# Two rope products written in place in PSUM, and the banks handed back after the rope sums, in a fused attention and feed-forward kernel

## The reference

```python
qkv = x @ w_qkv.T                              # 16 heads of 32
q = q * cos + _rotate_half(q) * sin            # the rope, the same for k
k = k * cos + _rotate_half(k) * sin
scores = jnp.einsum('bhqd,bhkd->bhqk', q, k) * scale
scores = jnp.where(keep, scores, -jnp.inf)     # 0 <= row - column < 64
out = jnp.einsum('bhqk,bhkd->bhqd', softmax(scores), v)
x = layernorm(x + out @ w_out.T)
gate = silu((x @ w_gate) * s_gate); up = (x @ w_up) * s_up
x = layernorm(x + ((gate * up) @ w_down) * s_down)
```

## Time and profile before

| what | value |
|---|---|
| time, median of 3 executions | 1167.32 us (1166.16 to 1168.19) |
| profiled execution, first to last instruction (its span) | 1164.2 us |
| median of the runs less the span | 3.1 us |
| PE busy | 1154.0 us, 99% |
| DVE busy | 984.6 us, 85% |
| POOL busy, ACT busy | 587.3 us, 584.4 us, 50% each |
| granted TensorE clock | 1.000 of full speed |

### The profile page before, as it was taken

How to read it: one execution, slowest core, us unless ns; L and a number is a source line. 1 busy time by engine, 2 the same in 40 slices (tenths; PEclk the granted TensorE clock), 3 DMA queues, 4 the chain that set the end, 5 groups by cost and what they waited for, 6 DMA issues and landing times.

```text
span 1164.2 us, 25539 instructions
## 1 busy us (share of the span) xinstructions
PE 1154.0 (99%) x8433; PEld 567.9 (49%) x8433; DVE 984.6 (85%) x2821; ACT 584.4 (50%) x1640; POOL 587.3 (50%) x563
## 2 busy tenths in 40 slices
PE   9999999999999999999999999999999999999998
PEld 4344446444464444644455444554445444464444
DVE  7899998898987899879998899897898988986434
ACT  3953883048820588105880169701686027950330
POOL 0775684156731667326771367613676236752330
PEclk9999999999999999999999999999999999999999
DMA  9999786366562765617656096561964537734000
GB/s 295 173 175 252 137 166 160 66 88 137 111 149 55 110 131 107 145 41 128 132 97 141 37 146 119 101 132 46 155 123 88 131 63 137 120 73 109 19 2 36
DMA packets 352077, 134.80 MB, mean 116 GB/s; under 512 B 309840, under 2 KB 332496, under 8 KB 351952
## 3 DMA queue, kind: packets, MB, share of 16 engines
q1 hardware_dynamic: 334976, 106.86, 49.6%
q0 software_dynamic: 10560, 17.30, 5.1%
q10 hardware_dynamic: 6416, 9.00, 2.1%
HBM read 32.19 MB, written 8.39 MB: 35 GB/s over the span
## 4 chain that ended last, share of the span: by engine, by line
PE 97%; DVE 1%; ACT 1%; issue 1%; POOL 0%; POOLq 0%; DVEq 0%
PE bank L842 61%; PE bank L1058 18%; PE bank L848 10%; PE bank L984 3%; PE bank L964 2%; PE bank L864 1%; PE bank L1080 1%; ACT bank L1243 1%; PE bank L873 0%; PE bank L1069 0%; PE bank L948 0%; DVE wd L1373 0%; ACT wu L1186 0%; DVE ffn_tmp L1530 0%; ACT fuse L1186 0%
## 5 line engine op out<-in xcount | busy, mean ns | idle before, releaser
L842 PE MATMUL bank<-x1T,wg 128*128 128x512 f16 (+1 forms) x1032 | 242.5, 378 | 0.0
L842 PE MATMUL bank<-x1T,wu 128*128 128x512 f16 x1024 | 241.9, 379 | 0.0
L1243 ACT ACTIVATE bank<-bank,neg_max,qk_scale 128x128 f32<-128x128 f32 x512 | 220.5, 435 | 7.8 <-DVE neg_max L1558 6.1
L1058 PE MATMUL bank<-wd,fuse 128*128 128x512 f16 (+2 forms) x1056 | 222.7, 373 | 0.0
L660 POOL TENSOR_TENSOR fuse<-ffn_tmp,fuse 128x512 f16<-128x512 f32 x128 | 149.7, 1170 | 117.5 <-ACT fuse L1186 116.8
L742 POOL TENSOR_TENSOR fuse<-fuse 128x512 f16<-128x512 f32 x116 | 137.7, 1218 | 74.9 <-ACT fuse L1186 72.8
L1058 PEld LDWEIGHTS bank<-wd,fuse 128*128 128x128 f16 x1056 | 101.9, 98 | 118.0
L842 PEld LDWEIGHTS bank<-x1T,wu 128*128 128x128 f16 x1024 | 100.1, 98 | 120.7
L655 POOL TENSOR_TENSOR xT_sb<-probs,xT_sb 128x512 f16<-128x512 f32 x112 | 129.6, 1158 | 44.5 <-ACT xT_sb L1186 44.4
L842 PEld LDWEIGHTS bank<-x1T,wg 128*128 128x128 f16 x1032 | 96.3, 98 | 113.9 <-issue 4.0
L1196 ACT ACTIVATE ffn_tmp<-bank,tanh_scale 128x512 f32<-128x512 f32 x128 | 88.2, 689 | 100.0 <-PE bank L842 76.8
(11 more groups left out here) (235 smaller groups left out, 1621.5 us busy)
## 6 DMA issues: line engine op xcount, KB each, us to landing
v_cross<-v_own SPq DMA_DIRECT2D x64, 128.0 KB, 2.4
out<-x ACTq DMA_DIRECT2D x31, 256.0 KB, 2.0
xT_sb<-xT SPq DMA_DIRECT2D x30, 256.0 KB, 4.1
qkT<-x SPq DMA_DIRECT2D x28, 256.0 KB, 3.8
wg<-w_gate POOLq DMA_DIRECT2D x7, 1024.0 KB, 5.2
wu<-w_up POOLq DMA_DIRECT2D x7, 512.0 KB, 6.0
wqkv<-w_qkvT SPq DMA_DIRECT2D x8, 256.0 KB, 6.3
wg<-w_gate POOLq DMA_DIRECT2D x1, 2048.0 KB, 8.4
```

Of the source, the lines that this page charges most:

```text
L842: last = pe.matmul(dst, lhsT, rhs, start=(i == 0), stop=(i == len(pairs) - 1))
L1058: last = pe.matmul(dst[:, cols], fuse[:, s, z, rows], wd[:, s, cols], start=(s == 0 and z == 0), stop=(s == STEPS - 1 and z == 1))
L1243: last = act.activation(unit, unit, ACT.Exp, bias=neg_max[:, s % 2, h // 3, h % 3:h % 3 + 1], scale=qk_scale[:, 2:3], accum_out=row_sum[:, ...
```

## The change

In tiles 1 to 7 (`ffn` true) the order of the four products becomes 3, 0, 1, 2. Products 3 (even * sin) and 1 (odd * sin) still go to SBUF. Products 0 (even * cos) and 2 (odd * cos) come second in their bank, and are written back over the bank that they read. The sums then read one bank and one SBUF place each and write to SBUF as before. So the banks are in use until the sums are done, and the three places on PE that waited for `rope_read` before they reuse a bank wait for `rope_done` now. Tile 0's own rope and its waits stay, and so does the wait of the DMA that loads new tables. The number of instructions stays.

```diff
@@ project_v
-                    wait(rope_read, pe, a, j // 2)
+                    wait(rope_done, pe, a, j // 2)
@@ scores
                 elif ffn:
-                    wait(rope_read, pe, a, 2 if s == 0 else NB - 1)
+                    wait(rope_done, pe, a, 2 if s == 0 else NB - 1)
@@ rope_products
                 for part in parts:
-                    i = (0, 3, 1, 2)[part]
+                    i = ((3, 0, 1, 2) if ffn else (0, 3, 1, 2))[part]
                     src = (even, odd, odd, even)[i]
-                    last = dve.tensor_tensor(free_view(place[i], heads), free_view(src, heads), table(i), ALU.mult)
+                    dst = src if ffn and part % 2 else place[i]
+                    last = dve.tensor_tensor(free_view(dst, heads), free_view(src, heads), table(i), ALU.mult)
@@ rope_sums
                 place = rope_place(j, ffn)
+                even, odd = qk_banks(j, ffn) if ffn else (place[0], place[2])
                 wait(rope_read, dve, a, j)
-                dve.tensor_tensor(place[0], place[0], place[1], ALU.subtract)
-                done(rope_done, dve.tensor_tensor(place[2], place[2], place[3], ALU.add))
+                dve.tensor_tensor(place[0], even, place[1], ALU.subtract)
+                done(rope_done, dve.tensor_tensor(place[2], odd, place[3], ALU.add))
```

## The result

The changed kernel takes 1170.81 us (median of 6 runs, 1169.29 to 1171.69) against 1166.88 us for the kernel before on the same chips (6 runs). The ratio is 1.0029, with a 95% interval of 1.0019 to 1.0040: slower by 2.2 to 4.7 us. The profiled execution has a span of 1169.1 us, 4.9 more than before.

What follows compares the result with a forecast made beforehand. The prediction took PE, busy 99% of the span, as the bound. It summed 2.2 (tile 0's end) + 0.1 (start of round 1) + 0 (rounds) = 2.3 us on 1167.3, giving 1169.6 us; range 1167.9 to 1171.2 us.

Steps and rivals of the forecast that it cites:

- PE bounds the rounds, and DVE's relief does not reach the end: Rounds: PE runs its own list, 141.92 us each; DVE's saving becomes idle time before the scores, no gain or cost.
- The rival with a faster kernel: Rounds: if DVE bounded them, up to 14.5 us would go less the 2.3, giving 1155.1 us; chance 0.05.
- The sums lose their tail: DVE's rope sums, seven tiles: with one bank operand they fall to about 0.69 us each, 14.5 us gone from DVE.
- Prices of bank operands: DVE's products written to banks and sums reading banks: 0 to 0.02 us an instruction, under 1.2 us in all.
- Tile 0's end: the one real wait: project_v of tile 1's block 0 waits for sums behind keep_o and two finish_x1: 2.21 us stall, lasting until the end.
- sums that stay stretched: Rival: scores 1 of round 1 waits 1.6 us, 3.8 in all, 1171.1 us; shares 0.11 with two other cases.
- The forecast's mechanism: Whole kernel: the stall at tile 0's end plus a little at round 1's start, 2.0 to 2.6 us; chance 0.76.
- the wait priced too low, in the case with 0.11: A PE wait costing more than forecast; no size given; chance 0.11 together with stretched sums or dear in-place writes.
- the border of 0.2%: Whole kernel: 0.2%, 2.3 us, about what measurement can tell from no change; within 0.48, slower 0.47, faster 0.05.
- Start of round 1: Scores 1 of round 1, one tile of seven: DVE's chain hangs on PE; 0 to 0.14 us lost, 0.1 taken.
- No stall in tile 0: Rival, tile 0's end: first two finish_x1 run before POOL's subtraction, project_v on time; 0 to 0.2 us, 1167.4; chance 0.08.

Runs made afterwards that it cites:

- experiment 6: Changed kernel, but block 0 of tile 1 keeps the old products and sums over SBUF and its rope_read hand-over: 1167.17 us, ratio 0.9998.
- experiment 7: Changed kernel with tile 1 block 0's rope sums directly behind their products and POOL's weight subtraction behind its first two split_low: 1166.86 us, ratio 0.9996.
- Experiment 2: Kernel before with only the three waits changed to rope_done, all products and sums over SBUF as before: 1171.45 us, ratio 1.0040.
- Experiment 3: Changed kernel with 11 extra matmuls on PE ahead of project_v of tile 1's block 0, result overwritten: 1169.27 us, ratio 1.0019.
- experiment 5: Changed kernel with the rope sums of tile 1's block 0 put between the two finish_x1 in DVE's list: 1168.96 us, ratio 1.0017.
- experiment 8: Changed kernel with 5 extra matmuls on PE ahead of project_v of tile 1's block 0: 1169.95 us, ratio 1.0024.
- experiment 1: Changed kernel with tile 1 block 0's rope sums directly behind their products, ahead of keep_o and the two finish_x1: 1167.34 us, ratio 0.9997.
- experiment 4: Changed kernel with POOL's weight subtraction in tile 0 moved behind its first two split_low of tile 1's block 0: 1167.37 us, ratio 1.0001.

## Why the prediction came out as it did

- **PE bounds the rounds, and DVE's relief does not reach the end.** Right. The rounds are the same 141.92 us, DVE's idle time before the scores' maxima grew from nothing to 1.93 us, and experiments 6 and 7 keep the relief and stay within 0.13% of the kernel before by their intervals. The rival with a faster kernel is out.
- **The sums lose their tail.** Right: 28 sums of each kind at 680 to 689 ns. Experiment 2, where they keep it, has the 1.6 us wait at scores 1 that the prediction priced at 1.6 for this rival. DVE as a whole got 12.0 us and not 14.5: the sums alone did shrink by 14.7, but other operations were stretched in turn, one split_x1 by 0.96 us and finish_x1 by 0.32. The other 1.4 us were not traced to their operations. Nothing of the time hangs on them.
- **Prices of bank operands.** Right: 5 ns for a product, nothing for a sum. The Trainium skill's figures for a PSUM source ("VectorE: DVE Perf Modes", section on the TRN2 errata) gave an estimated 0.065 us more for each sum, and that is not seen: 689 and 680 ns with a bank, 693 and 683 as the medians without.
- **Tile 0's end: the one real wait.** The place, the cause and the first part of the price were right: 2.2 us forecast, 2.42 measured. finish_x1 took 3.59 us in place of 3.27, and the passage from DVE to PE about 0.05 us (sums done at 92.97, project_v at 93.02) in place of the 0.14 that was taken for it; the two errors offset in part.
- **The term that was missing.** The forecast carried the stall to the end as it stood. It left out what the standstill does to PE itself: 1.70 us for the project_v behind it, on the lower clock. Of the ledger's 4.46 us that is 38%. This is the main reason why the kernel came out 3.9 us over the kernel before and not 2.3. Experiments 3, 5 and 8 each take the lower clock away, in two ways, and 1.7 to 1.8 us go with it between project_v and weigh_v 15. The trace before did show a fall, but where it costs nothing: at its end, 4.4 us after the last matmul, the granted clock goes to 0.50. No matmul at the lower clock stood in it from which to price one. The Trainium skill says it in words ("TensorE: Matmul & The Clock Gate", Part 1): the gate passes only part of the pulses by default, and PE's own activity releases it. The trace after agrees with 0.50 behind the gap. It should have been weighed as a rival.
- **The range held partly by luck.** Its upper end, 1171.2, was put there for sums that stay stretched, and they did not. The forecast with the 1 us that was given to the spread of the runs ends at 1170.6, and 1170.81 lies above that. The forecast's mechanism alone was given 2.0 to 2.6 us with a chance of 0.76, and the loss was 3.9; it belongs to the wait priced too low, in the case with 0.11. The forecast also started from 1167.3, and the kernel before has a median of 1166.88 here, which hides 0.4 us of the miss. Against the border of 0.2% that the prediction names, the ratio of 1.0029 is slower, the outcome that it held for slightly the less likely of the two (0.47 to 0.48); the interval's lower end, 1.0019, just touches the border.
- **Start of round 1.** Forecast 0 to 0.14 us, measured 0.34. The step that failed is that DVE's chain hangs on PE there. Before, DVE waited 0.23 us for PE at 109.84. After, it did not wait at all: a `split_x1` on DVE, a pass over two SBUF tensors, took 1.64 us in place of 0.68 beside one of POOL's split_low, and the chain ran 0.28 us later against PE than before. In experiment 1 that operation took 0.68 and scores 1 lost 0.10; in experiments 4 and 7 it took 1.64 and 1.65, and scores 1 lost 0.33 and 0.34. DVE meets POOL there within less than 0.1 us, and which of the two goes first decides about 0.25 us. Where DVE's operation began 0.05 us ahead of POOL's (before, 106.39 and 106.44; experiment 1, 106.96 and 107.01) it took 0.68. Where it began 0.06 or 0.07 us behind (after, 110.63 and 110.56; experiments 2 to 8 alike) it took 1.64 or 1.65.
- **No stall in tile 0**, the rival on the other side: its condition did not come up in the changed kernel, and experiment 4, which makes it true, gives the time that it named, 1167.4 us.

Open: how long PE must stand still before it costs the clock. The ends of the traces speak against a fixed length. There PE stands still after its last matmul, and the clock falls 2.0 us later in experiment 5, 3.0 in 1, 4.4 in the kernel before and 5.3 in the changed kernel. In tile 0 it fell 2.9 us after PE had stopped (changed kernel) and 3.5 us (experiment 2), both times with PE at work again. So a gap of 2.35 us may be spared in another execution, and one of 2 us may not. Two of the changed kernel's six executions have spans of 1167.5 and 1167.6, and the other four 1168.9 to 1169.4. That would fit a fall that does not come each time, but no trace of the short ones shows it.

## What to carry to other kernels

When a buffer's release moves from the last reader's first half to a later instruction on the same engine, read what stands between the two in that engine's list, at every place where they are called: the rounds had 0.9 us of slack or more, and the hand-written end of tile 0 had none. Price a new PE gap twice, as its own length and as the slower work behind it if the granted clock falls (1.7 us here), and remember that shortening such a gap a little can give back more than its own length. An engine that is relieved gains nothing while another one runs its list without idling.

## What the runs showed of the hardware

- The gaps of 2.35 us (changed kernel) and 2.96 us (experiment 2) on PE, after tens of microseconds of nearly full work, were followed by a granted clock of about 0.50 and a project_v of 5.40 us; the gaps of 1.06 and 1.85 us (experiments 8 and 5) were followed by 1.00 and 3.70 us, and that of 1.63 us before scores 1 in experiment 2 by 1.00. The clock fell only after work had begun again: 0.90 in the window from 92 to 94, 0.50 from 94 to 96. These are single profiles of each, and they set no threshold: after the last matmul the clock fell 2.0 us later in one trace and 5.3 in another.
- Removing 0.50 us of gap (experiment 5) removed 2.2 us of PE's path from weigh_v 14 to weigh_v 15 in its profile, and the kernel lies 2.3 us less over the kernel before by the medians.
- A DVE tensor_scalar with one SBUF tensor source and an SBUF output, both fp32, was held until POOL's subtraction had ended: 3.59 us for two beside it, 1.08 for two without it (experiment 4); in experiment 5 the one beside it took 3.08 us, from 87.50 to 90.58, and POOL's ran from 87.92 to 90.28. DVE's sums and split_x1 over two SBUF tensors are stretched beside POOL too, to as much as 1.64 us. The operations over one SBUF tensor and one bank that were looked at are not: 120 rope products at 673 to 692 ns, and the 28 sums of each kind in the changed kernel at 679 to 693 and 676 to 682.
